# Opening and routing placed beside the first feed-forward, GpSimd's additions moved into the first heads, block rows loaded first, no swapped rope weights

## The reference

```
x = x + 0.5 * ffn0(layernorm(x))      # dense 256x256 + 8 low-rank experts, top 2
x = x + attn0(layernorm(x))           # 16 heads of 16, q/k/v/o with low-rank updates
x = x + 0.5 * ffn0(layernorm(x))
x = x + 0.5 * moe(layernorm(x))       # 32 experts, top 4 of given indices, silu(g) * u
x = x + attn1(layernorm(x))           # latent attention, 16 heads, rope on 64 dims, causal
x = x + 0.5 * moe(layernorm(x))
```

## Time and profile before

| | us |
|---|---|
| median of 3 runs | 1730.48 (1728.32 to 1732.19) |
| the profiled execution | 1720.4, its span 1718.5 |
| opening, to the start of `first_layer` | 0 to 53 |
| `first_layer` before the heads | 53 to 143 |
| heads of the first attention | 143 to 545 |
| rest of the second feed-forward, scatters, first loads | 545 to 633 |
| experts, first time | 633 to 795 |
| gathering, weights, first latent preparation | 795 to 870 |
| latent attention | 870 to 1510 |
| experts, second time | 1510 to 1718.5 |

### The profile page before, as it was taken

The page is one execution under the profiler, slowest core; times in us unless marked ns, Lnnn a source line. Parts: engine busy times, 40 slices in busy tenths (PEclk is TensorE's granted clock), DMA queues, the critical chain, the costliest instruction groups (busy, mean ns, idle before and its releaser), DMA issues. The chain is left out here.

```text
span 1718.5 us, 20953 instructions
## 1 busy us (share of the span) xinstructions
PE 1255.5 (73%) x5976; PEld 764.1 (44%) x5976; DVE 899.9 (52%) x2519; ACT 631.2 (37%) x1670; POOL 557.3 (32%) x628
## 2 busy tenths in 40 slices
PE   2445888796886229996279859985996699379990
PEld 1222334333232128885135534552564355368880
DVE  7514667675763202224768637844883487112227
ACT  0111354453544015554025503530552156045550
POOL 0253564352313315553022103311430232335550
PEclk9776789898989559998579968995998699789995
DMA  9743706035023055455200000000000000135447
GB/s 307 256 76 53 93 29 78 7 82 79 32 117 148 40 192 163 158 164 174 86 0 1 1 0 22 19 10 4 23 22 4 9 23 19 43 123 163 157 142 256
DMA packets 105217, 145.08 MB, mean 84 GB/s; under 512 B 14436, under 2 KB 87301, under 8 KB 104085
## 3 DMA queue, kind: packets, MB, share of 16 engines
q1 hardware_dynamic: 87701, 101.74, 23.0%
q0 software_dynamic: 17408, 42.00, 6.9%
HBM read 77.31 MB, written 63.00 MB: 82 GB/s over the span
## 5 line engine op out<-in xcount | busy, mean ns | idle before, releaser
L150 POOL DMA_INDIRECT outs_dram<-m_ys,dest x192 | 184.4, 960 | 183.6 <-ACT m_ys L929 182.4
L598 DVE TENSOR_REDUCE a_mx<-a_psU 128x1 f32<-128x512 f32 x256 | 164.1, 683 | 124.9 <-PE a_psU L363 123.5
L949 DVE TENSOR_TENSOR m_hm<-m_psG,m_sg 128x128 f32<-128x128 f32 x192 | 56.0, 292 | 310.0 <-ACT m_sg L923 310.0
L1213 ACT ACTIVATE a_pr<-a_psA,a_nb 128x512 f32<-128x512 f32 (+3 forms) x256 | 132.2, 526 | 221.8 <-DVE a_nb L1333 221.8
L993 PE MATMUL m_psG<-arena,m_xgT 128*128 x768 | 204.1, 389 | 0.3
L468 ACT ACTIVATE a_P<-a_psS 128x512 f32<-128x512 f32 x256 | 143.3, 596 | 100.5 <-PE a_psS L374 97.7
L1145 PE MATMUL a_psA<-a_kT,a_q 128*128 128x512 f32 (+3 forms) x512 | 175.5, 459 | 5.2 <-ACT a_pr L1213 5.2
L1261 POOL TENSOR_TENSOR a_q<-a_q,a_t 64x512 f32<-64x512 f32 x64 | 80.7, 1262 | 258.1 <-DVEq L1317 133.6
L1344 DVE TENSOR_SCALAR a_pr<-a_pr,a_rec 128x512 f32<-128x512 f32 (+3 forms) x256 | 144.7, 585 | 6.8
L984 PE MATMUL m_psX<-ident,m_xg 128*128 128x128 f32 x384 | 74.6, 278 | 95.3 <-DMA m_xg<-rows_dram 95.3
L993 PEld LDWEIGHTS m_psG<-arena,m_xgT 128*128 128x128 f32 x768 | 132.4, 192 | 15.1 <-issue 2.6
(11 more groups left out here) (224 smaller groups left out, 2147.0 us busy)
## 6 DMA issues: line engine op xcount, KB each, us to landing
m_xg<-rows_dram SPq DMA_DIRECT2D x48, 512.0 KB, 4.3
rows_dram<-xd SPq DMA_DIRECT2D x8, 1536.0 KB, 12.0
arena<-in_mo_w SPq DMA_DIRECT2D x6, 2048.0 KB
arena<-part_dram SPq DMA_DIRECT2D x48, 256.0 KB
m_xg<-outs_dram SPq DMA_DIRECT2D x16, 512.0 KB, 4.3
m_ys<-outs_dram SPq DMA_DIRECT2D x16, 512.0 KB, 4.8
part_dram<-a_part SPq DMA_DIRECT2D x16, 384.0 KB, 2.5
a_V<-a_qf SPq DMA_DIRECT2D x1, 3072.0 KB
```

Of the source, the lines that this page charges most:

```text
L150: pool.indirect_dma_start(out=rows_dram, out_offset=bass.IndirectOffsetOnAxis(ap=slot[:, c:c + 1], axis=0), in_=row, in_offset=None).then_ ...
L598: dve.tensor_reduce(mx[g % 2][:, 4 * kt + qt:4 * kt + qt + 1], psU[n % 2][:, :], AX, ALU.max).then_inc(u_free, 1)
L1213: ins = act.activation(pr[s % 2][:, AT[t]:AT[t] + (t + 1) * P], psA[:, AT[t]:AT[t] + (t + 1) * P], ACT.Exp, bias=nb[s % 2][:, t:t + 1], sc ...
```

## The change

`start_stage` and `clear_after` go. Their work is done inside `first_layer`:

- SP loads batch 0 of `x`, the feed-forward's weights and the identity first (`first_loads`), then the other batches in one transfer, then the rest. ScalarE issues the four routing loads. The first feed-forward of batch 0 waits only for `first_loads`, and computes the statistics of its batch alone; those of the other batches follow at `p = F1 + 7`.
- One-hot (`p = F1 + 1`) and counting products (`F1 + 5`) stand in iteration -2, and ScalarE copies the counts from PSUM to SBUF (eight copies of 512 columns). The scan (`F1 + 7`) and the block bases (`F1 + 12`) are in iteration -1, on VectorE. The remaining additions over 2048 columns are GpSimd's, in iteration 0 (`route`). `place` is computed at the start of iteration 1, and the 64 scatters of the table move to iterations 1, 2 and 3 (22, 21, 21).
- The weight updates are four products in iteration -2 and four in iteration -1. The zeros go out as 12 transfers of 1 MB in iterations 0 and 1, from an 8 KB wide tile; `early` waits for them and goes out in iteration 2.
- `V` is filled by GpSimd (two memsets) instead of by a transfer. Batch 0's terms are split by VectorE.
- Order of `qk` is now query, key, query, key (eight heads each), and the parts are stored and loaded in halves of eight heads: 24 loads a batch, half as large. A group waits for its own half.
- The three rows of a group's maxima are issued by ScalarE, at the fourth point of the next group.
- `bias` of batch `i` comes in iteration `i`, behind the first set. Of the last batch's scatters only the last set is waited for.
- `moe_stage` loads the first two groups of blocks, then the latent weights, then the other groups.
- `latent_stage`: two query products a pair. The sine product is taken from the same PSUM bank in two instructions a head, each reading 32 partitions and writing the 32 next to them, with the sign moved into `la.sin`.

The diff, cut to what the text speaks of:

```diff
@@ first_layer, TensorE
+            def count():
+                pe.wait_ge(hot_ready, 1)
+                for q in range(CHUNKS):
+                    c = slice(q * 512, (q + 1) * 512)
+                    if q >= 2:
+                        pe.wait_ge(drained, q - 1)
+                    pe.matmul(psU[q % 2][:, :], oneb, hot[:, c], start=True, stop=True)
+                    pe.matmul(psS[q % 2][:, :], lessb, hot[:, c], start=True, stop=True).then_inc(counted, 1)
...
-                if g % 4 == 0 and c == 0 and qt == 0:
-                    pe.wait_ge(terms_in, 16 * 12 * (g // 4 + 1))
+                if g % 2 == 0 and c == 0 and qt == 0:
+                    pe.wait_ge(terms_in[g // 2 % 2], 16 * 12 * (g // 4 + 1))
@@ first_layer, ScalarE
+            def max_rows(g):
+                act.wait_ge(mpart_ready, g + 1)
+                o = (g // 4 % 2) * SLOT + (g % 4) * HPG * L
+                for t in range(3):
+                    act.dma_start(QS[NT + t:NT + t + 1, o:o + HPG * L], mpart[:, t * P:(t + 1) * P]).then_inc(max_in, 16)
+
             def side(i, p):
+                g = 4 * i + p // 8
+                if p % 8 == MAXROWS and live(g - 1):
+                    max_rows(g - 1)
@@ first_layer, VectorE
+                if i == -1 and p == QT:
+                    absorb(0, 4)
+                    first_rows(1)
+                if i == -1 and QK < p <= QK + 4:
+                    terms(p - QK - 1)
+                if i == -1 and p == QK + 2:
+                    absorb(4, 8)
+                if i == -1 and p == F1 + 7:
+                    scan()
+                if i == -1 and p == F1 + 12:
+                    dve.tensor_scalar(weight[:, :], weight[:, :], 0.5, None, ALU.mult)
+                    bases()
+                if i == 1 and p == 0:
+                    places()
@@ first_layer, GpSimd
-            pool.wait_ge(pads_in, 32)
+            step(pool.memset(V[:, :], 0.0))
...
-                pool.wait_ge(placed[b % 2], 16 * (b // 2 * TPB * TOPK + hi))
+                if b < B - 1 or hi == TPB * TOPK:
+                    pool.wait_ge(placed[b % 2], 16 * (b // 2 * TPB * TOPK + hi))
...
-            entry(0, 16)
...
-                if 0 <= b < B:
-                    bias(b)
+                if 1 <= b < B:
                     for c in range(4):
                         terms(b, c)
...
-                    if 0 <= i < 2:
-                        entry(16 + 24 * i + 8 * q, 24 + 24 * i + 8 * q)
+                    if i == 0:
+                        route(q)
+                    if i in (1, 2, 3):
+                        n = 22 + 21 * (i - 2)
+                        entry(n + 7 * q if i > 1 else (0, 8, 15)[q], n + 7 * q + 7 if i > 1 else (8, 15, 22)[q])
+                    if q == 0 and 0 <= i < B:
+                        bias(i)
@@ moe_stage, SP
-            if latent is not None:
-                for dst, src in latent.loads:
-                    sp.dma_start(dst, src).then_inc(latent.loaded, 16)
             for h in range(2):
                 sp.wait_ge(placed[h], 16 * TPB * TOPK * B // 2)
             for g in range(NX):
                 load(g)
+            if latent is not None:
+                for dst, src in latent.loads:
+                    sp.dma_start(dst, src).then_inc(latent.loaded, 16)
             for g in range(NX, NGRP):
                 load(g)
@@ latent_stage, VectorE (the whole of the new queries)
+                    n, h = U_P + 2 * c + part, 2 * c + part
                     ready(n)
+                    if c >= 2:
+                        dve.wait_ge(a_done, NBK * (b * H1 + h - 3))
+                    dve.tensor_tensor(q[h % 4][:, :], psU[:, :], la.cos[:, part * L:(part + 1) * L], ALU.mult)
+                    o = (c % 2) * L
+                    for lo in (64 * part, 64 * part + 32):
+                        to = lo + 32 if lo == 64 * part else lo - 32
+                        ins = dve.tensor_tensor(t2[to:to + 32, o:o + L], psU[lo:lo + 32, :], la.sin[lo:lo + 32, :], ALU.mult)
+                    ins.then_inc(u_free, 1)
...
                 for s in range(H1):
                     maxima(s, 0)
-                    if s < H1 - 2 and s % 2 == 0:
-                        queries(s // 2 + 1, 0)
+                    if s < H1 - 2:
+                        queries(s // 2 + 1, s % 2)
                     for k in range(1, NBK):
                         maxima(s, k)
                     divide(s, 0)
-                    if s < H1 - 2:
-                        queries(s // 2 + 1, 2 if s % 2 else 1)
                     for k in range(1, NBK):
                         divide(s, k)
```

More of the change, by code:

```diff
@@ L239, in first_layer, with scratch @@
         KS = ring[:, SLOT:2 * SLOT].bitcast(BF16)
+        W, CHUNKS = NE * NC, NE * NC // 512
+        free = 2 * SLOT
+        def scratch(cols, dt=F32):
+            nonlocal free
+            t = ring[:, free:free + (cols if dt != BF16 else cols // 2)]
+            free += cols if dt != BF16 else cols // 2
+            return t if dt == F32 else t.bitcast(dt)
+        counts, cums, run, hot = scratch(W), scratch(W), scratch(W), scratch(W, BF16)
+        lessb, oneb, one, idxf0 = scratch(P, BF16), scratch(P, BF16), scratch(1), scratch(NC)
+        lowi, highi = scratch(NC, I32), scratch(NC, I32)
+        start, cnt, nbf, bend, off = (scratch(NE) for _ in range(5))
+        cnti, past, owners, owner = scratch(NE, I32), scratch(NE), scratch(1), scratch(1, I32)
+        assert free <= 3 * SLOT
+        zero, place = run, dest[:, 0:NC]
+        lora_b, lora_a = (ring[0:16, SLOT // 2 + i * 4 * D:SLOT // 2 + (i + 1) * 4 * D] for i in range(2))
+        upper, idx = ring[:, 8 * D:8 * D + P], ring[:, 8 * D + P:8 * D + P + NC].bitcast(I32)
+        number = sb("number", [P, NC], I32)
+        ec = lambda t: t.rearrange("p (e c) -> p e c", c=NC)
         fxT = sb("fxT", [P, TPB * D])
@@ L457, in side @@
                     act.activation(ex[:, :], gap[:, :], ACT.Exp).then_inc(ex_ready, 1)
+                if i == -2 and p == F1 + 5:
+                    for q in range(CHUNKS):
+                        act.wait_ge(counted, q + 1)
+                        c = slice(q * 512, (q + 1) * 512)
+                        act.copy(counts[:, c], psU[q % 2][:, :])
+                        act.copy(cums[:, c], psS[q % 2][:, :]).then_inc(drained, 1)
             for i, p in points:
@@ new lines, in one_hot, with absorb @@
+            def one_hot():
+                dve.wait_ge(route_in, 16 * 4)
+                link(dve.tensor_copy(idxf0, idx))
+                dve.tensor_scalar(lessb, upper, -1.0, None, ALU.add)
+                dve.tensor_tensor(ec(hot), idxf0.unsqueeze(1).to_broadcast([P, NE, NC]),
+                                  iota[:, 0:NE].unsqueeze(2).to_broadcast([P, NE, NC]), ALU.is_equal).then_inc(hot_ready, 1)
+            def absorb(lo, hi):
+                if lo == 0:
+                    dve.wait_ge(rest_in, 16 * NREST)
+                    dve.tensor_scalar(bias_qk[:, 0:KD], bias_qk[:, 0:KD], HD ** -0.5, None, ALU.mult)
+                for n in range(lo, hi):
+                    k, c = ABSORB[n]
+                    dve.wait_ge(absorbed, n + 1)
+                    w = wt[:, (k * 4 + c) * D:(k * 4 + c + 1) * D]
+                    dve.scalar_tensor_tensor(out=w, in0=ab_bank(n), scalar=0.5, in1=w, op0=ALU.mult, op1=ALU.add).then_inc(kept, 1)
@@ new lines, in places, with scan @@
+            def places():
+                dve.wait_ge(slots_ready, 1)
+                dve.tensor_scalar(lowi, slot[:, :], P - 1, None, ALU.bitwise_and)
+                link(dve.tensor_scalar(highi, slot[:, :], 7, None, ALU.logical_shift_right))
+                dve.scalar_tensor_tensor(out=place, in0=lowi, scalar=float(NBLK), in1=highi, op0=ALU.mult,
+                                         op1=ALU.add).then_inc(place_ready, 1)
+            def scan():
+                dve.wait_ge(drained, CHUNKS)
+                dve.tensor_tensor_scan(run, one[:, 0:1].to_broadcast([P, W]), counts, 0.0, ALU.mult, ALU.add).then_inc(scanned, 1)
@@ new lines, in bases @@
+            def bases():
+                dve.wait_ge(scanned, 1)
+                dve.memset(start[:, 0:1], 0.0)
+                link(dve.tensor_copy(start[:, 1:NE], ec(run)[:, 0:NE - 1, NC - 1]))
+                link(dve.tensor_tensor(cnt, ec(run)[:, :, NC - 1], start, ALU.subtract))
+                link(dve.tensor_scalar(cnti, cnt, float(P - 1), None, ALU.add))
+                link(dve.tensor_scalar(cnti, cnti, 7, None, ALU.logical_shift_right))
+                link(dve.tensor_copy(nbf, cnti))
+                link(dve.tensor_tensor_scan(bend, one[:, 0:1].to_broadcast([P, NE]), nbf, 0.0, ALU.mult, ALU.add))
+                link(dve.tensor_tensor(off, bend, nbf, ALU.subtract))
+                dve.scalar_tensor_tensor(out=off, in0=off, scalar=float(P), in1=start, op0=ALU.mult,
+                                         op1=ALU.subtract).then_inc(based, 1)
```

(9 more changed lines are left out.)

415 lines of the change are left out of this document (181 added, 234 removed).

## The result

The changed kernel takes 1680.9 us (median of 4 runs, 1674.8 to 1681.7) against 1729.4 for the kernel before (4 runs, 1728.1 to 1732.2): a ratio of 0.971, 95% interval 0.9684 to 0.9736. It is faster by 48.5 us. Forecast were 72, and 1658 with a range of 1615 to 1702. So the sign and the range held, and a third of the gain is missing.

What follows compares the result with a forecast made beforehand. No engine bounds the whole kernel, a series of stages with a serial chain before the heads. Terms -63, +14, -12 and -11 sum to -72 us, from 1730.5 to 1658; range 1640 to 1680 from its terms, 1615 to 1702 with rivals.

Steps and rivals of the forecast that it cites:

- Opening, -63: From the start to the first maximum: that maximum moves from 143.2 to 80 us, 63 us less.
- Heads, +14: Attention heads, tail included: 20 us of waits removed, 5 and 32 added, 3 saved at the tail; 14 us more.
- Waits for the maxima's rows, -20: Heads: TensorE's three waits for small rows queued behind SP's loads of terms go, 20.0 us less.
- GpSimd late, +32: Heads: ScalarE waits for GpSimd's late split of the maxima, 4, 16, 2, 8 and 2 us; bounds 0 and 75.
- The tail, -3: End of the heads: two of three waits between the last batch's scatters go, 1.5 us each.
- Start of the experts, -12: Expert stage: first block 17.6 us earlier, then a stall of 6; 12 us less, bounds -17.6 and -6.
- Latent heads, -11: Latent stage: a pair takes 11.9 us instead of 12.40, first heads start later; 11 us less, bounds -28 and +25.
- Never late: Rival: GpSimd is never late, so the heads change by -18 and not +14; 1626 us, chance 0.15.
- Late by 75: Rival: scatter waits of 10 us and more under clears and experts make GpSimd late by 75; 1701 us, chance 0.05.
- VectorE as the bound of the pair: Rival, latent stage: ScalarE's exponentials fall behind VectorE's queries; pair 13.8 us, +39 and not -11, 1708 us, chance 0.12.
- the opening's inserted work shows in full: Rival: all work inserted before the first maximum shows in the time; 1675 us, chance 0.10.
- The 32-partition products: Rival, latent stage: products writing to other partitions take 1.37 us and not 0.68; 1735 us, chance 0.03.

Runs made afterwards that it cites:

- early_gated: The changed kernel with the first two loads of expert weights (4 MB) held back until the scores of nine groups are done: 1663.2 us, 0.9598.
- after_again: The changed kernel, unchanged, run and profiled once more as a reference: 1681.3 us.
- before_again: The kernel before, unchanged, profiled once more: 1728.0 us in its one run, span 1726.0.
- entries_moved: The changed kernel with the table's 64 scatters dealt out 36, 7 and 21 over three batches instead of 22, 21 and 21: 1658.9 us, 0.9639.
- latent_first: The changed kernel with the latent weights' loads issued before the first loads of block rows again: 1678.5 us, 0.9681.
- sine_one: The changed kernel with one 64-partition sine product per latent head instead of two of 32, leaving out the swap of rope halves: 1651.8 us, 0.961.
- rows_late: The changed kernel with ScalarE issuing the three rows of the maxima six eighths into the group, not three eighths: 1660.6 us, 0.956.
- spread: The changed kernel with the 13 latent loads issued two at a time behind the third and later loads of block rows: 1668.6 us, 0.9637.

## Why the prediction was right, and where its size was off

**Opening, -63: right**, measured -66. VectorE starts the first maximum behind the block bases, as forecast. This is read from the timeline; no run undoes a part of the new opening. The fill of V is one GpSimd memset of 5.2 us at 1.2, which nobody waits for.

**Heads, +14: the term that was mis-sized; measured +46.0 and +1.1 behind them.** By its parts:

- Waits for the maxima's rows, -20: right. Two of the three stretches in which they fell shrank by 5.6 and 6.0. The third, with the wait of 9.9, is the one that grew most; its 9.9 are taken as gone, since after has 0.4 us of such waits in all.
- ScalarE's 48 issues, +5: nearly nothing. They take 0.61 us each as a median, 29 us in all, and the eight stretches without another cause grew by 2.1 together.
- GpSimd late, +32: its waits are 38.5, in three places (7.5, 21.2, 9.8) and not five. The mechanism and the iterations are those forecast; the longest was 21.2 and not 16, since its scatters landed after 13.5 us and not the 10.8 or 6.7 of the earlier trace rows, and early_gated shows the 9.3 of it that are the expert weights.
- Not in the sum at all: what follows a wait. The three stretches grew by 9.0, 13.6 + 9.9 and 15.6, that is 48.1 and not 38.5. Windows of after across the longest wait and behind it:

```profile
330.50:352.90 22.40, 0.26 (x3) 0.02 (x1) 0.49 (x1) 1.16 (x3) 6.86 (x10) 0.57 0.84 255
352.90:361.10 8.20, 8.12 (x32) 4.57 (x33) 1.38 (x2) 1.91 (x4) 5.24 (x7) 0.72 0.02 1
361.10:370.40 9.30, 7.99 (x38) 1.97 (x36) 8.60 (x24) 4.95 (x10) 5.33 (x6) 1.00 0.25 86
```

TensorE did nothing for 22 us and was granted 0.57, mostly the lower of its two levels. The next 8.2 us are all work, granted 0.72, and only then comes 1.00. So a wait on this path can cost more than its length, here by a quarter. The second pair of profiles makes that much less: after_again has 46.7 us of such waits, and against before_again the three stretches grew by 39.3 + 9.3, that is 48.6. Between 2 and 10 us follow the waits, and two profiles don't settle it.

- Set to nothing: GpSimd's routing additions "lie in idle time". They do for GpSimd. But VectorE's same 47 instructions of that stretch are busy 22.1 us instead of 17.0: +5.1. Six small ones of the expert gate hold all of it. The timeline of VectorE in before:

```profile
180.94 0.16 DVE L547 TENSOR_TENSOR a_gap<-a_top 128x4 f32<-128x4 f32 x1
...
182.66 0.16 DVE L493 TENSOR_SCALAR a_den<-a_ex 128x4 f32<-128x4 f32 x1
```

and of GpSimd and VectorE in after:

```profile
111.23 4.50 POOL L769 TENSOR_TENSOR arena<-arena 128x2048 f32<-128x2048 f32 x1
...
114.63 1.12 DVE L697 TENSOR_TENSOR a_gap<-a_top 128x4 f32<-128x4 f32 x1
...
115.91 3.65 POOL L770 TENSOR_TENSOR arena<-arena 128x2048 f32<-128x2048 f32 x1 [0.18 <-POOL arena L769]
...
117.32 2.26 DVE L561 TENSOR_SCALAR a_den<-a_ex 128x4 f32<-128x4 f32 x1
```

Each of the two ends as a GpSimd addition ends (115.75 and 115.73, 119.58 and 119.56). That is 3.1 of the 5.1. The other 2.0 are four instructions beside GpSimd's additions of the bias (119.7 to 122.5), which the change moved here. The reductions from PSUM kept their 0.68. My own sum for the latent stage used this contention; here I left it out.
- Three more stretches grew by 5.5, 3.4 and 3.4. The growth of the first went with entries_moved; its cause, and the other two, stay open.
- The tail, -3: the two waits did go, from the last batch's first scatter to its last it is 20.5 us and not 22.5. But its first scatter came 3.1 later behind the last exponential.

The heads together: -21.5 + 48.1 + 5.1 + 12.2 + 2.1 = 46.0.

**Start of the experts, -12: right in size, wrong in its split.** Measured -12.1: -20.5 to the first block, then a stall of 4.45 (forecast 6) and a slow clock around it, together 8.4. From the stage's first load to its first block 22.0 became 4.0, so 18.0 less where the forecast had 17.6. Another 2.5 lie ahead of that load, which comes 5.6 us behind the last scatter in all 12 profiles of changed kernels and 8.1 in both of the kernel before. Why stays open. latent_first shows that the order itself is worth 4 to 7; the rest came with these 2.5 and with less to load. I had taken all as one.

**Latent heads, -11: right**, measured -11.8; the pair is 11.73 (forecast 11.9). The first pair of each batch went the other way, from 11.6 to 12.2 before to 12.6 to 13.4, 4 us in all (forecast 3). Between the batches 3 us more came back. The rule weighed in the forecast can be read directly now. From start to start, the maximum to the cosine product is 0.60, the cosine product to the first sine product 0.70. In sine_one that last step is 0.61 where the sine product starts at partition 0 like the cosine product (1030.36 to 1030.97), and 0.70 where it starts at 64. So a move to another group of partitions costs 0.1, as the forecast had it. The rule of the Trainium skill (VectorE: DVE Perf Modes, Two Vector instructions with no wait between them) agrees. From the last sine product to the next maximum it is 0.82 to 0.84 with either start; there the program waits for the product to end, 0.2 us a head that the forecast had not seen apart.

**The rivals.** "Never late" is refuted by the 38.5 us. "Late by 75" was too much, but its cause is the one that was under-priced, and the result lies between it and the forecast. VectorE as the bound of the pair: it is the bound (sine_one), but at 11.73 and not 13.8, and not by the rival's mechanism, since VectorE waits for ScalarE's exponentials 1.8 us in all, in eight places. That the opening's inserted work shows in full is refuted by its -66. The 32-partition products take 0.69 us, not 1.37.

**On the queues.** The waits of the earlier trace rows go when ScalarE issues the rows, and yet in rows_late 12 KB of them, in a queue of their own, kept TensorE waiting 5.8 us under clears. The Trainium skill (DMA: Bandwidth & Descriptors, DMA queue model, Arbitration) has each DMA engine take turns between queues, a packet at a time. Both fit: another queue saves what stands ahead in the first one, and not the turns.

## What to carry to other kernels

When an engine gets a wait at a fixed point in its order, add up the queue of the engine that it waits for, at that point, with every scatter's landing under the heaviest transfer that can run then. Ask which transfers have no hurry: two loads that nobody needed for 200 us cost 9. Then allow for what follows a wait on the path of the matrix engine (here 2 to 10 us behind 39 to 47 us of waits), and price additions on GpSimd as time of VectorE's small instructions beside them.

## What the runs showed of the hardware

- A DMA issue is cheap on the engine that issues: 0.61 us as a median on ScalarE, 0.43 for most on SP. The 1.0 of the earlier trace rows was a mean with a few long issues in it, one of 6.0. It depends on the place in a burst and not on the transfer alone: the issue for `la_down` took 0.43 us in before, 6.85 in after and 2.03 in spread, where the loads go out two at a time.
- Six row scatters land in 3.8 us behind their issue without the 4 MB beside them and in 13.5 with them (11.5 in after_again).
- A small VectorE instruction can stand until GpSimd's addition ends: 2.26 us instead of 0.16 for 4 columns.
- A scan of 2048 columns took 4.42 us, a comparison into 2048 columns of bf16 2.28.
- The same kernel's profiled executions differ by 5 to 8 us in span, in several stages at once; a difference of 10 us between two traces is not a mechanism yet.
